# Attention: the turn of the probabilities moved from TensorE to a DMA round trip and VectorE

## The reference, cut to what matters

```python
# x: 16 batches of 256 rows of 512; layer 0 ahead of this (convolution, routed experts)
kv_c = kv @ W_kvc;  q_c = q @ W_dq
q_nope, q_rope = (q_c @ W_uq), rope(q_c @ W_qr)          # 16 heads
k_nope, v, k_rope = (kv_c @ W_uk), (kv_c @ W_uv), rope(kv_c @ W_kr)
scores = (q_nope . k_nope + q_rope . k_rope) * scale      # 256 x 256 a head
scores = where(seg - 8 <= key <= seg, scores, -1e30)
attn = softmax(scores)
out = (attn @ v) @ W_o ;  x = x + out
x = x + gelu(layernorm(x) @ proj1.T + b1) @ proj2.T + b2  # the dense block
```

## Time and profile before

| | |
|---|---|
| median of 3 runs | 3065.67 us (3062.55 to 3068.54) |
| the profiled execution | 3065.81 us, span 3064.0 us |
| TensorE (PE) busy over the span | 3032.5 us, 99% |
| VectorE (DVE) busy | 2248.4 us, 73% |
| ScalarE (ACT) busy | 1379.9 us, 45% |
| GpSimd (POOL) busy | 1224.1 us, 40% |
| first scores product, last product of the attention | 1037.0 us, about 2355 us |
| one batch of the attention, in its middle | 81.73 us, 5.108 us a head |

### The profile page before, as it was taken

How to read it: one execution, slowest core, us unless ns; L and a number is a source line. 1 busy time by engine, 2 the same in 40 slices (tenths; PEclk the granted TensorE clock), 3 DMA queues, 4 the chain that set the end, 5 groups by cost and what they waited for, 6 DMA issues and landing times.

```text
span 3064.0 us, 50062 instructions
## 1 busy us (share of the span) xinstructions
PE 3032.5 (99%) x18181; PEld 2636.4 (86%) x18181; DVE 2248.4 (73%) x5504; ACT 1379.9 (45%) x3399; POOL 1224.1 (40%) x1190
## 2 busy tenths in 40 slices
...
GB/s 153 131 144 138 129 130 86 86 307 299 220 265 284 189 49 49 49 49 43 49 42 49 49 49 36 49 38 47 49 29 81 88 56 55 55 49 43 46 42 14
DMA packets 179011, 292.41 MB, mean 95 GB/s; under 512 B 22616, under 2 KB 73952, under 8 KB 178768
## 3 DMA queue, kind: packets, MB, share of 16 engines
...
## 4 chain that ended last, share of the span: by engine, by line
PE 92%; DVE 3%; DMA 2%; POOL 1%; ACT 1%; issue 1%; SPq 0%; POOLq 0%; DVEq 0%
PE f_Y L559 4%; PE t_U L1818 4%; PE f_Y L560 4%; PE f_Y L562 4%; PE t_U L1819 4%; PE t_U L1820 4%; PE g_O L2640 4%; PE g_PH L2628 4%; PE g_PH L2627 4%; PE g_PH L2626 4%; PE g_O L2642 4%; PE g_O L2641 4%; PE t_T L1794 3%; PE f_Y L554 2%; PE t_PO L1804 2%; PE t_PO L1805 2%
## 5 line engine op out<-in xcount | busy, mean ns | idle before, releaser
L1954 ACT ACTIVATE t_pr<-t_sm,t_nb 128x256 f32<-128x256 f32 x512 | 256.7, 502 | 418.5 <-DVE t_nb L2176 418.5
L2372 POOL TENSOR_TENSOR t_r<-t_r 128x256 f32<-128x256 f32 x128 | 95.8, 749 | 696.7 <-DVE t_r L2155 387.5
L2696 DVE CAST g_hh<-g_hf 128x512 fp32r<-128x512 f32 x128 | 67.8, 530 | 382.0 <-PE g_O L2642 380.2
L2667 ACT ACTIVATE g_hf<-g_PH,b1g 128x512 f32<-128x512 f32 x128 | 88.1, 688 | 528.3 <-PE g_PH L2628 457.0
L1360 POOL TENSOR_TENSOR c_kf<-c_vt,c_ct 128x512 f32<-128x512 f32 x256 | 284.5, 1129 | 5.9 <-ACT c_vt L775 3.2
L2186 DVE TENSOR_SCALAR t_pr<-t_pr,t_rw 128x256 f32<-128x256 f32 x512 | 256.7, 501 | 18.1
L559 PE MATMUL f_Y<-c_kh,c_th 128*128 128x512 f32 x540 | 250.8, 465 | 0.0
L562 PE MATMUL f_Y<-c_kl,c_th 128*128 128x512 f32 x540 | 213.7, 396 | 0.7 <-DVE c_kl L1072 0.7
L560 PE MATMUL f_Y<-c_kh,c_tl 128*128 128x512 f32 x540 | 213.4, 395 | 0.0
L2640 PE MATMUL g_O<-g_w,g_hh 128*128 128x512 f32 x512 | 200.1, 391 | 5.0 <-DVE g_hl L2698 5.0
L1818 PE MATMUL t_U<-t_voh,t_oth 128*128 128x512 f32 x512 | 202.0, 394 | 0.0
...
## 6 DMA issues: line engine op xcount, KB each, us to landing
xs<-c_zero SPq DMA_DIRECT2D x71, 256.0 KB, 4.6
...
ys<-f_yt ACTq DMA_DIRECT2D x71, 256.0 KB, 5.1
f_xg<-xn SPq DMA_DIRECT2D x40, 256.0 KB, 4.9
c_xt<-x SPq DMA_DIRECT2D x32, 256.0 KB, 3.5
c_cr<-ctx SPq DMA_DIRECT2D x32, 256.0 KB, 4.0
c_ct<-ctxh SPq DMA_DIRECT2D x32, 256.0 KB, 4.9
c_t<-kt SPq DMA_DIRECT2D x32, 256.0 KB, 5.0
```

## The change

For each head the probabilities now leave ScalarE's queue for a DRAM buffer fp, in 512-byte pieces, and come back in another order; VectorE transposes 32x32 blocks. Part by part:

- TensorE's `pturn` is gone (four transposes a head), and with it its bank: `av` now alternates between two banks. `av` stands four heads behind the scores instead of two, `vo` six instead of four.
- The scaling of the probabilities moves from VectorE to ScalarE (`normalise`, one head behind), which writes them in groups of 32 columns. VectorE keeps the two reciprocals (`inverses`).
- ScalarE issues the store (`probabilities_out`) and, later in the same step, the load (`probabilities_in`), which waits for that store to have landed.
- VectorE transposes (`pturn`, three heads behind) into `ptq`; ScalarE makes the hi part from SBUF instead of PSUM, and the lo part moves from VectorE to GpSimd.
- Loads of 512 KB are cut into pieces of 128 or 256 KB at different steps; the store of x3 moves from GpSimd to SP and is cut into four; the store of x2 moves from SP to GpSimd; GpSimd's mixing is spread over the steps h = 11 to 14.
- The first dense product of the first block moves up into the attention's last steps, and in the first dense group SP issues the rows' transfers two blocks earlier. Six products on the identity in step 2 (`keep_busy`) are dropped. The first three blocks of dense weights are split two steps later.

The core of the diff:

```diff
+    with ExitStack() as low:
+        m.ptq = sb(nc, low, "t_ptq", [128, 2, 2, 256])
     m.ptl = t("ptl", [128, 2, 2, 256], F32R)
...
-    m.pr = t("pr", [128, 2, 2, 256])
+    m.pr = t("pr", [128, 2, 4, 2, 2, 32])
+    m.pq = t("pq", [128, 2, 512])
...
-    m.S, m.T, m.PO = (bank(nc, ctx, f"t_{n}") for n in ("S", "T", "PO"))
+    m.S, m.T, m.PB = (bank(nc, ctx, f"t_{n}") for n in ("S", "T", "PO"))
+    m.PO = (m.T, m.PB)
...
+def turned_rows_of(ap, c):
+    return ap.rearrange("(t u c) l -> u c t l", t=2, c=4)[:, c, :, :]
+
...
-    def load(b):
+        sp.dma_start(m.cT[:, k, :], d["ctxb"][b][:, k, :]).then_inc(*Q["tct"]("ct", b, k))
+
+    def load(b, t):
         w.wait_ge(*P["pmx", 2 * b - 1])
-        w.wait_ge(*Q["tx2"]["x2", b - 1])
-        sp.dma_start(m.xt[:, :, :], halves_of(d["xa"][b])).then_inc(*Q["tx"]("xa", b))
-        if b > 1:
-            context(b)
+        w.wait_ge(*Q[kept(b - 1)]["x2", b - 1])
+        sp.dma_start(m.xt[:, t, :], halves_of(d["xa"][b])[:, t, :]).then_inc(*Q[f"tx{t}a"]("xa", b, t))
 
...
+    def store(b):
+        w.wait_ge(*V["add", 2 * b + 1])
+        for c in range(4):
+            sp.dma_start(turned_rows_of(d["x3"][b], c), m.xo[32 * c:32 * c + 32, :, :]).then_inc(*Q["to"]("out", b, c))
...
-    def pturn(N):
-        w.wait_ge(*V["nm", 2 * N + 1])
-        w.wait_ge(*V["vw", 4])
-        w.wait_ge(*V["ptl", N - 1])
-        for kb in range(2):
-            for t in range(2):
-                i = pe.transpose(m.T[:, 256 * kb + 128 * t:256 * kb + 128 * t + 128], m.pr[:, N % 2, t, 128 * kb:128 * kb + 128], ident)
-        i.then_inc(*P("pt", N))
...
-        o = m.PO[:, 256 * (N % 2):256 * (N % 2) + 256]
-        w.wait_ge(*V["ptl", N])
+        o = m.PO[N % 2][:, 0:256]
+        w.wait_ge(*G["ptl", N])
...
-        if 1 <= N <= TOTAL:
-            pturn(N - 1)
-        if 2 <= N <= TOTAL + 1:
-            av(N - 2)
+        if 4 <= N <= TOTAL + 3:
+            av(N - 4)
-        if N == 2:
-            keep_busy(pe, m.PU[0], ident, 6)
+        if N == TOTAL + 3:
+            dense_first(pe, w, K, 0, 0)
...
-            w.wait_ge(*P["pt", N - 2])
             w.wait_ge(*V["rc", x - 4])
-            ac.activation(m.pr[:, N % 2, t, :], m.sm[:, k4, :], ACT.Exp, bias=m.nb[:, k4, 0:1], scale=-1.0,
+            ac.activation(m.sm[:, k4, :], m.sm[:, k4, :], ACT.Exp, bias=m.nb[:, k4, 0:1], scale=-1.0,
                           accum_out=m.rw[:, k4, 0:1]).then_inc(*A("ex", x))
 
+    def normalise(N):
+        w.wait_ge(*Q[f"ps{N % 2}"]["ps", N - 2])
+        for t in range(2):
+            x, k4 = 2 * N + t, (2 * N + t) % 4
+            w.wait_ge(*V["rc", x])
+            ac.activation(m.pr[:, N % 2, :, :, t, :], m.sm[:, k4, :].rearrange("p (i k f) -> p i k f", i=4, k=2), ACT.Copy,
+                          scale=m.rw[:, k4, 1:2]).then_inc(*A("nm", x))
+
+    def probabilities_out(N):
+        w.wait_ge(*A["nm", 2 * N + 1])
+        w.wait_ge(*V["pt", N - 4])
+        ac.dma_start(K.d["fp"][N % 4].rearrange("(i p f) -> p i f", i=4, f=128),
+                     m.pr[:, N % 2, :, :, :, :].rearrange("p i k t f -> p i (k t f)")).then_inc(*Q[f"ps{N % 2}"]("ps", N))
+
+    def probabilities_in(N):
+        w.wait_ge(*Q[f"ps{N % 2}"]["ps", N])
+        w.wait_ge(*V["pt", N - 2])
+        ac.dma_start(m.pq[:, N % 2, :], K.d["fp"][N % 4].rearrange("(p l) -> p l", p=128)).then_inc(*Q[f"pl{N % 2}"]("pl", N))
+
     def pturn(N):
-        w.wait_ge(*P["pt", N])
-        w.wait_ge(*P["av", N - 2])
-        copy(m.pth[:, N % 2, :, :], m.T[:, :].rearrange("p (k c) -> p k c", k=2)).then_inc(*A("pth", N))
+        w.wait_ge(*V["pt", N])
+        copy(m.pth[:, N % 2, :, :], m.ptq[:, N % 2, :, :]).then_inc(*A("pth", N))
...
+        if 5 <= N <= TOTAL + 4:
+            av(N - 5)
+        if 1 <= N <= TOTAL:
+            normalise(N - 1)
+            probabilities_out(N - 1)
         if N < TOTAL:
             exps(N)
+        if 3 <= N <= TOTAL + 2:
+            pturn(N - 3)
+        if 1 <= N <= TOTAL:
+            probabilities_in(N - 1)
...
-    def normalise(N):
+    def inverses(N):
         for t in range(2):
             x, k4 = 2 * N + t, (2 * N + t) % 4
             w.wait_ge(*A["ex", x])
-            w.wait_ge(*V["nm", x - 4])
             ve.reciprocal(m.rw[:, k4, 1:2], m.rw[:, k4, 0:1]).then_inc(*V("rc", x))
-            w.wait_ge(*V["rc", x])
-            ve.tensor_scalar(m.pr[:, N % 2, t, :], m.pr[:, N % 2, t, :], m.rw[:, k4, 1:2], None, ALU.mult).then_inc(*V("nm", x))
 
     def pturn(N):
-        w.wait_ge(*A["pth", N])
-        ve.tensor_tensor(m.ptl[:, N % 2, :, :], m.T[:, :].rearrange("p (k c) -> p k c", k=2), f32(m.pth[:, N % 2, :, :]),
-                         ALU.subtract).then_inc(*V("ptl", N))
+        w.wait_ge(*Q[f"pl{N % 2}"]["pl", N])
+        w.wait_ge(*P["av", N - 2])
+        ve.transpose(m.ptq[:, N % 2, :, :].rearrange("p k q -> p (k q)").rearrange("p (k c t) -> p c k t", k=4, c=4),
+                     m.pq[:, N % 2, :].rearrange("p (c k f) -> p c k f", c=4, k=4)).then_inc(*V("pt", N))
 
...
         if N < TOTAL:
             maxima(N)
+        if 3 <= N <= TOTAL + 2:
+            pturn(N - 3)
+        if N < TOTAL and N % 2 and (N + 1) // 2 < TOTAL // 2:
+            qabs((N + 1) // 2)
+        if 5 <= N <= TOTAL + 4:
+            av(N - 5)
+        if N < TOTAL:
             if r == 3 and 4 * (q4 + 2) < TOTAL:
                 qrot(q4 + 2, 0)
             if r == 0 and 4 * (q4 + 1) < TOTAL:
                 qrot(q4 + 1, 1)
-        if N >= 4 and (N - 4) % NH == NH - 1:
-            add_rows((N - 4) // NH)
+            inverses(N)
...
+    def pturn(N):
+        w.wait_ge(*A["pth", N])
+        gp.tensor_tensor(m.ptl[:, N % 2, :, :], m.ptq[:, N % 2, :, :], f32(m.pth[:, N % 2, :, :]), ALU.subtract).then_inc(*G("ptl", N))
...
-        if g + 1 < GROUPS and 6 <= k < 10:
-            dense_rows_out(sp, w, K, 4 * (g + 1) + k - 6)
-        if g + 1 < GROUPS and 7 <= k < 11:
-            dense_rows_in(sp, w, K, 4 * (g + 1) + k - 7)
+        r = k + 2 if g == 0 else k
+        if g + 1 < GROUPS and 6 <= r < 10:
+            dense_rows_out(sp, w, K, 4 * (g + 1) + r - 6)
+        if g + 1 < GROUPS and 7 <= r < 11:
+            dense_rows_in(sp, w, K, 4 * (g + 1) + r - 7)
```

More of the change, by code:

```diff
@@ L1625, in sync_attention @@
     sp.dma_start(m.wqr[:, 1, :], d["wqrb"]).then_inc(*Q["tw1"]("rb"))
-    context(1)
+    for k in range(4):
+        context(1, k)
     factors(6)
@@ L1631, in sync_attention @@
     factors(9)
-    load(1)
+    load(1, 0)
+    load(1, 1)
     segment(1)
-    for N in range(TOTAL + 4):
+    for N in range(TOTAL + 8):
         b, h = divmod(N, NH)
-        if N >= 4 and (N - 4) % NH == (12 if N - 4 < NH else 8):
-            residual((N - 4) // NH)
+        if N >= 7 and (N - 7) % NH == NH - 1:
+            store((N - 7) // NH)
+        if 6 <= N < TOTAL + 2:
+            for c in range(4):
+                if (N - 6) % NH == (11 if N - 6 < NH else 8) + c:
+                    residual((N - 6) // NH, c)
         if N < TOTAL and b + 2 < B:
-            if h == 10:
-                load(b + 2)
+            if h in (9, 11):
+                load(b + 2, h // 11)
+            if 3 <= h < 7:
+                context(b + 2, h - 3)
             if h == 14:
                 segment(b + 2)
-                keep(b + 2)
         if N + EARLY + 2 < NH:
@@ L1852, in tensor_attention @@
     weights(7)
-    for N in range(TOTAL + 4):
+    for N in range(TOTAL + 6):
         b, h = divmod(N, NH)
@@ L1911, in turned @@
         if b >= PARTS:
[L1912 removed]
+            w.wait_ge(*Q["to"]["out", b - 2, 3])
             w.wait_ge(*V["wdql"])
```

165 lines of the change are left out of this document (85 added, 80 removed).

## The result

The changed kernel takes **3155.75 us** (median of 3, 3149.84 to 3158.58) against 3065.67: ratio 1.0291, 95% interval 1.0262 to 1.0319, slower by 90 us. The forecast was 3009, the range 2940 to 3095: both wrong, and the sign too.

A forecast was written before the change was run, and what follows sets the result against it. The prediction took TensorE's work to bound the middle batches, then ScalarE's list with TensorE's uneven steps: 14 batches x 3.7 = 52 us, plus 5 us in the dense block, 57 off 3065.8, giving 3009 us, range 2940 to 3095.

The forecast's parts named there:

- ScalarE's sum: ScalarE's list in the attention: 3.92 us a head, 74.8 us a batch, above TensorE's 72.9, with 2.4 us for the landing.
- the slope: At ScalarE's load behind its store: each 0.1 us of longer landing costs 22 us in all.
- the tipping point: At ScalarE's load: the gain is gone at 0.26 us more landing, 2.66 us on the mean, a batch of 82.1.
- bad end: GpSimd's lo part, late beside the mixing at h = 11 to 14: 2 us a batch, 28 us in all, at worst.
- The slack of 3 us: TensorE needs GpSimd's lo part in av one step later, some 3 us of slack, so lateness was priced at nothing.
- 78.0: Forecast time in us of a middle attention batch, 3.7 less than before, from ScalarE's and TensorE's lists and other transfers.
- TensorE's floor: TensorE's work in a middle batch without the transposes: 81.7 - 8.8 = 72.9 us, at 0.55 us a head.
- the rival of 2936 us: TensorE keeps the pace in the attention, ScalarE's wait hidden, a batch 72.9 to 74; chance 0.24 for everything below 2980.
- the dense rows: First dense group: SP issuing the rows' transfers two blocks earlier takes 5.0 us off, nothing if waits move to the fetches.
- The drain at the end: End of the attention, pipeline two heads deeper: TensorE fills it with other products, so zero, 3 us either way.
- the landing binds, and the kernel is slower: At ScalarE's load behind its store: 3143 us at a mean landing of 3.0; chance 0.20 for everything above 3065.
- the one for GpSimd: GpSimd's late lo parts stop TensorE 2 us a batch: 3037 us; chance 0.12 for 3045 to 3065, with a 2.6 us landing.

The follow-up runs named there:

- e10: The changed kernel with ScalarE's load put ahead of the hi part instead of behind it: 3275.5 us.
- e2: The changed kernel with GpSimd's mixing spread over one more step: 3123.6 us.
- e11: The changed kernel with ScalarE's load issued one step later, in its old place behind the exponentials: 3096.6 us.
- e5: The changed kernel with GpSimd's mixing spread over one more step and ScalarE's load one step later, behind the exponentials: 3053.4 us.
- e9: The kernel before the change, with TensorE's four transposes of the probabilities issued twice for each head: 3175.3 us.
- e14: The study's best kernel (3031.3 us) with SP's store of a batch's rows listed as one piece a step: 3040.8 us.
- e16: The changed kernel with SP's list paced, waiting ahead of each step for the exponentials of the head before in batches 1 to 13: 3145.6 us.
- e13: The changed kernel with SP's four row-store pieces listed one at each of steps h=6 to 9, instead of all at h=6: 3151.3 us.
- e15: The changed kernel with each of the four pieces of a finished batch's rows stored a second time, to dead rows: 3175.6 us.

## Why the prediction was wrong

- **The step that failed: the landing's mean.** ScalarE's sum was 2.4 us for the landing and 0.14 x 1.0 x 16 = 2.2 us a batch for other transfers, "of that I take 0.9", so 2.46 on the mean. It measured 2.86. Its other terms held: scalings 0.51 each, 0.90 for the pair (0.92), the load's issue 0.33, the store's 0.38. The median landing was 2.33, and it is 2.34 in the heads that no other packet meets. I had the slope (22 us for 0.1; e10 measured 0.86 of it) and the tipping point at 2.66 (2.72, counted from the 2.46 of the sum), and the earlier trace rows showed 3.4 and 3.9 beside other traffic; I priced a list that stands at each landing by a median, and by a DMA share of 0.14 taken from the kernel before. In the changed kernel that share is 0.48, since the probabilities themselves go out and come back, and more than half of the heads have another transfer of SP or GpSimd near them. The Trainium skill's estimate (DMA: Bandwidth & Descriptors, Anatomy of one DMA), stated for GpSimd's path, is 2.6 us; the quiet landing here is below it and the mean above.
- **GpSimd's mixing, priced at nothing**, cost 32 us (e2), 2.3 a batch: my "bad end" of 2. The slack of 3 us was counted by steps; a list of 7.5 us in a step of 5.4 uses it up. I had no term for the clock, which is 0.50 to 0.72 on the mean of 5 us behind 18 of TensorE's 21 waits of 2.5 us and more between 1140 and 2290 us.
- **The size of the landing's part is smaller than my slope says.** 78.0 + 0.40 x 16 + 2.3 = 86.7 us a batch, measured 86.8, but this fit is luck. With the whole wait off ScalarE's list, and not only its excess, a batch fell by 2.9 us (e11), and by 3.2 with the mixing spread (83.9 in e2, 80.7 in e5). So of the 8.8 us a batch above the forecast some 3 are the landing's, 2.3 to 2.9 the mixing's, and 2.7 stay when both are gone. For these 2.7 the forecast had no term: TensorE's floor (below) can be up to 1.8 of it, and the rest is open.
- **TensorE's floor** was 72.9, and is 74.7 (e9). In the earlier trace rows I read 0.55 us from the first transpose's weights to those of the next product; in the timeline of TensorE's products the four take 0.35 from start to start. It puts the rival of 2936 us out of reach: with 256 x 0.435 = 111 us and 7 of the dense rows the time comes to 2947 at best.
- **The drain at the end, priced at zero, 3 us either way**: 17.3 us were lost behind the last batch's keys, although the dense rows won 7 there. Moving the load a step later gave 13.3 of them back (e11), so most of this too is ScalarE standing at the landing. The lo part on VectorE and the fetches ahead of the row store gave 13.7 and 8.4, of which 2 and 7 behind the last batch's keys.
- **VectorE** 58.7 us a batch (62.4: the block transpose takes 0.706 and not 1.08), **GpSimd** 45.8 (46.6), the dense rows 7 us (5): right or near, and neither engine binds by its sum.
- The outcome is the rival "the landing binds, and the kernel is slower" (3143 at a mean of 3.0), to which I gave 0.20, joined by the one for GpSimd. They were cases side by side; in the chip they added up. The 3143 is near the measured 3155.8 in part by luck, since it leaves out the mixing and prices the landing by the full slope.
- **Open**: why another packet in flight lengthens a landing by one to three microseconds, and by so little beside SP's loads of rows; changing a burst, cutting others and pacing SP left the mean within 0.06 us, and q8's packets were not touched. Also untested is a wait that the kernel before doesn't have: ScalarE's copies to t_xo stand at SP's row store for 43.7 us over 13 batches in e5, 3.4 a batch. And open is where the 9.5 us of e14 come from beyond the wait named, and the 10 us of e16.

## What to carry to other kernels

An engine that issues a transfer and then waits for it in its own list pays each landing's excess over the work laid under it: add it up with the mean landing beside the traffic that the change itself brings, or issue the second half a whole step later, which here was worth 59 us for one line. What more waiting costs does not tell what less of it gives back: here 0.86 of it one way and about 0.3 the other, since another list takes over. When work moves to an engine with room in the sum, look at its fullest step: 7.5 us of list in a step of 5.4 cost 32 us although the engine was half idle. In this kernel turning by DMA pays once no list waits for the landing and the mixing is spread; with the two edits behind that it gives 1.1%, of which the dense rows alone are 0.2, where the transposes' whole cost is 3.6 (111 us).

## What the chip showed beyond that

- With no other packet in flight, the load that waits for a store of 256 KB in 512-byte pieces goes out 2.34 us after the store on the mean of 120 heads, 2.73 at most; beside SP's row store 4.5 to 4.9 on the mean (changed kernel, e13, e15, e16).
- Packets of q8, a queue of the kind "instruction" to which no engine of this kernel issues transfers, show in this: 3.34 us on the mean of the 18 heads whose store met only such a packet.
- VectorE's 32 by 32 block transpose of 128 x 512 takes 0.706 us here and 1.080 in the earlier trace rows, where it writes with another stride.
- Four transposes of 128 columns cost TensorE 0.435 us when it has no wait, though each is 0.27 long in the trace.
